# A decoder layer on one core: half of the last pair's value projection moved between that pair's scores, with w_out's loads spread behind its parts

## Chip, cores and metric

One core of one Trainium2 chip. The metric is the device time of one execution in microseconds; three runs of the kernel before gave a median of 2648.34 us (2646.84 to 2651.65).

## What is computed

Per batch of four (1024 tokens, 1024 channels): a layer norm, causal self-attention with 16 heads of 64, a residual; a layer norm and a cross-attention over a context; a residual; a layer norm and a gated low-rank step; a residual. The first part, cut:

```python
qkv = layernorm(x) @ w_qkv                      # 1024 -> 3 x 1024
scores = einsum('bqhd,bkhd->bhqk', q / 8, k)    # causal mask
attn = softmax(scores)
x = x + einsum('bhqk,bkhd->bqhd', attn, v) @ w_out
x = x + cross_attention(layernorm(x), ctx, Wq, bq, Wk, bk)
x = x + gated_low_rank(layernorm(x), ...)
```

## The kernel before, in words

**Work and names.** Heads are taken two at a time: eight pairs p = 0 to 7 per batch, n = 8b + p over all. Each number is split into two fp16 halves, so a product is three matmuls (`three`, lines 559 to 566). Each engine walks a list of steps written out by hand: `PE_BODY` and its like for pairs 0 to 6, `PE_TAIL` and its like for pair 7 and all that follows it in the batch (lines 41 to 93). A `+` behind a step means that it belongs to the next pair (or batch), a `-` to the one before. `walk` (lines 306 to 326) goes through them; `ONCE` adds single steps, among them `JI0 JI1 KI` behind T6 of pair 6 of each batch (line 139).

**The steps spoken of.** `P t h part` is a quarter of a projection (t: 0 query, 1 key, 2 value; h: the half of the tokens; six 512-column matmuls, lines 570 to 592) that reads the turned input `xt` in array `r1`. `CH`/`CL` take the finished bank out of PSUM on ACT (line 776) and DVE (line 914). `V` (lines 455 to 460, SP) is the DMA transpose of the value half-pair rows into `vn`. `S q` are the scores of query block q (PE, lines 608 to 630), `X q` their maximum (DVE, 915 to 928), `E q j` the exponentials of head j (ACT, 792 to 803), `R q` one over their sum (DVE, 929 to 936), `H q j`/`L q j` the two fp16 halves of the probabilities (POOL 1196 to 1204, DVE 937 to 942), `T q` the DMA transpose of block q's probabilities, 4(q+1) blocks of 128x128 (SP, 445 to 454). `M0`/`M1` multiply the turned probabilities with the values, for query blocks 0 to 3 and 4 to 7 (PE, 631 to 653); `OH`/`OL` take the result out. `OI i` loads a quarter (1 MB) of w_out into `wo`, which is the same memory as `xt` (SP, 506 to 513). `KI` loads the cross-attention's weights (512 KB) into memory that is also the projection weights' (SP, 514 to 516); `KH`, `KL` split them (828 to 830, 1100 to 1103). `JI` loads a quarter of the context (512 KB, 517 to 524), `JH`/`JL` split it, `G` projects it (683 to 692), `QH`/`QL` take that out. `B` is the output projection (703 to 720).

**Order around the change.** All DMAs of these steps are issued by SP, one after another, on one queue. In pair 6's body PE ends with `P200+ P201+ P202+ P203+ P210+ P211+ P212+ S0+ S1+ P213+`; SP ends with T6, JI0, JI1, KI, T7, V+. KI waits until all 48 banks of the batch are projected (line 515). In the tail PE goes `S2 S3 M1- S4 G0 S5 G1 M0 S6 G2 B00 S7 ...`, and SP `OI0 OI1 T0 T1 OI2 T2 OI3 JI2 T3 T4 JI3 ...`. The waits that set the order:

```python
sp.wait_ge(part_ok, 6 * PAIRS * (b + 1))      # 507, OI: all banks projected
sp.wait_ge(l_ok, 2 * (TB * n + q) + 2)        # 447, T: both low halves of q
if q >= PARTS + 2: sp.wait_ge(m_ok, 2 * n + 1)
elif q < PARTS and n > 0: sp.wait_ge(m_ok, 2 * n)   # 450-451: M1 of the pair before
pe.wait_ge(t_in[s], 16 * (4 * n + 2 * g + 2)) # 634, M0: T0 to T3; M1: T0 to T7
pe.wait_ge(v_in, 16 * (n + 1))                # 635, M0: this pair's V
```

Of the kernel before, what the change touches and what calls it, by code (L numbers as in the profile page):

```python
# [14 lines left out]
P = 128  # L15
# [13 lines left out]
PARTS = 4  # L29
# [28 lines left out]
"""  # L58

PE_TAIL = """  # L60
    S2 S3 M1- S4 G0 S5 G1 M0 S6 G2 B00 S7 G3 B01 B10 B11 M1 B20 N0 B21 N1 B30 N2 B31 N3 B40 N4 B41 N5 B50 N6 B51 N7
    B60 B61 B70 B71 Z00 Z01 Z10 Z11 Z20 Z21 F0 Z30 Z31 F1 D0 Z40 Z41 F2 D1 U0 Z50 Z51 F3 D2 U1 Z60 Z61 F4 D3 U2
    Z70 Z71 F5 D4 U3 P000+ P001+ P002+ P003+ P010+ P011+ P012+ P013+ F6 D5 U4 P100+ P101+ P102+ P103+ P110+ P111+
    P112+ P113+ F7 D6 U5 P200+ P201+ P202+ P203+ P210+ P211+ P212+ P213+ D7 U6 S0+ S1+ U7
"""
DVE_TAIL = """
    X0 L70- L71- CL21 R0 X1 L00 L01 X2 R1 L10 L11 R2 X3 KL JL0 R3 OL1- X4 L20 L21 QL0 JL1 R4 L30 L31 X5 L40
    L41 QL1 JL2 R5 OL0 X6 L50 L51 R6 QL2 JL3 X7 L60 L61 R7 QL3 RA0 L70 L71 RA1 LB0 OL1 CX0 LL0 LB1 CR0 RA2 CX1 CLO0
    LB2 CR1 CX2 LL1 CLO1 CR2 RA3 CX3 CLO2 LB3 CR3 CX4 CLO3 CR4 RA4 CX5 CLO4 LB4 CR5 CX6 CLO5 CR6 RA5 CX7 CLO6 LB5
    CR7 CLO7 RA6 LB6 AB0+ AB1+ AL0+ RA7 LB7 AL1+  # L70
# [3 lines left out]
    WLO7 Y6 CL21+ Y7  # L74
"""
ACT_TAIL = """
    E00 E01 CH21 E10 E11 E20 E21 KH JH0 E30 E31 OH1- QH0 JH1 E40 E41 E50 E51 QH1 JH2 OH0 E60 E61 QH2 JH3 E70 E71
    QH3 LX0 OH1 CE0 LX1 CE1 CE2 CE3 LX2 CE4 CE5 CE6 CE7 AX0+ AX1+ AX2+ TX0 LX3 AX3+ TX1
    LX4 AX4+ TX2 GE0 LX5 AX5+ TX3 GE1 WHI0 LX6 AX6+ TX4 GE2 WHI1 LX7 AX7+ TX5 GE3 WHI2 TX6 GE4 WHI3 TX7 GE5 WHI4
    CH00+ CH01+ GE6 WHI5 CH10+ CH11+ GE7 WHI6 CH20+ WHI7 CH21+  # L80
# [5 lines left out]
    AH6+ TS4 AS7+ TH4 LH7 AH7+ TS5 TH5 TS6 TH6 TS7 TH7  # L86
"""
SP_TAIL = """
    OI0 OI1 T0 T1 OI2 T2 OI3 JI2 T3 T4 JI3 T5 RI0 T6 RI1 T7 WD0+ WD1+ WD2+ RI2 RI3 CT0 LT0 CT1 RI4
    LT1 RI5 CT2 CT3 RI6 CT4 CT5 RI7 CT6 CT7 AI0+ AI1+ AI2+ AT0+ AT1+ AI3+ LT2 AT2+  # L90
    TT0 AI4+ LT3 AT3+ TT1 AI5+ LT4 AT4+ AI6+ TT2 LT5 AT5+ AI7+ TT3 LT6 YO0 AT6+ TT4 LT7 YO1 AT7+ TT5
    YO2 TT6 YO3 TT7 YO4 WD0++ YO5 WD1++ YO6 V+ YO7
# [58 lines left out]
def decoder_layer(nc, x, w_qkv, w_out, ctx_t, w_ctx, b_ctx, w_ffn, v_ffn, w_up, center, slope, out):  # L151
    es = ExitStack()
    with es:
# [88 lines left out]
        with ExitStack() as s4:  # L242
# [30 lines left out]
        w_ld = [sem(f"w_ld{t}") for t in range(3)]  # L273
        wo_st = [sem(f"wo_st{s}") for s in range(2)]
        part_ok, ch_ok, c_ok, v_in = sems("part_ok ch_ok c_ok v_in")
        s_ok, peak_ok, low_ok, e_ok, den_ok, r_ok, h_ok, l_ok = sems(
            "s_ok peak_ok low_ok e_ok den_ok r_ok h_ok l_ok")
        t_in = [sem(f"t_in{s}") for s in range(2)]
# [26 lines left out]

        def walk(engine, attend, rest):

            for kind, args, off in starts[engine]:
                if kind in OF_PAIR:
                    attend(kind, args, off - 1)  # L310
                else:
                    rest(kind, args, 0)
            for n in range(BATCH * PAIRS):
                b, p = divmod(n, PAIRS)
                for kind, args, off in (tails if p == PAIRS - 1 else bodies)[engine]:
                    if kind in OF_PAIR:
                        m = n + off
                        if p == 0 and off == 0 and kind in ("CH", "CL"):
                            continue
                        if m // PAIRS == b or p == PAIRS - 1 and 0 <= m < BATCH * PAIRS:  # L320
                            attend(kind, args, m)
                    elif b + off < BATCH:
                        rest(kind, args, b + off)
                    if off == 0:
                        for once, which, _ in steps(ONCE.get((engine, n, kind + "".join(map(str, args))), "")):
                            rest(once, which, n // PAIRS)
# [90 lines left out]
        with nc.Block() as block:  # L417

            @block.sync
            def _(sp):  # L420
# [49 lines left out]
                def rest(kind, a, b):  # L470
# [12 lines left out]
                    if kind == "AI":  # L483
                        if b > 0:
                            if i < 2:
                                sp.wait_ge(n_lo, TB * b)
                            else:
                                sp.wait_ge(a_lo, T - 1)
                        sp.dma_start(x_in(T), x[b, i]).then_inc(a_in[T % 2] if b > 0 else a_first[i], 16)
                    elif kind == "AT":  # L490
                        sp.wait_ge(a_lo, T + 1)
                        if b > 0:
                            sp.wait_ge(out_mm, TB * b)
                        sp.dma_start_transpose(xt[:, :, :, :].rearrange("p s k q -> p (s k) q")[:, :, block_of(i)],
                                               xh1[:, T % 2, :, :].rearrange("p s d -> p (s d)")
                                               ).then_inc(xt_in[T % 2], 16)
                    elif kind == "VI":
                        if i == 0:
                            sp.wait_ge(scan_ok, 12)
                        else:  # L500
                            sp.wait_ge(wo_ok, i)
                        sp.dma_start(wo_raw, w_out[i]).then_inc(wo_in, 16)
                    elif kind == "VS":
                        sp.wait_ge(wo_ok, i + 1)
                        sp.dma_start(wo_pairs[:, :, i, :], wo16[:, i % 2, :, :]).then_inc(wo_st[i % 2], 16)
                    elif kind == "OI":
                        sp.wait_ge(part_ok, 6 * PAIRS * (b + 1))
                        if b == 0:
                            for s in range(2):
                                sp.wait_ge(wo_st[s], 64)  # L510
                        sp.dma_start(wo[:, :, 2 * i:2 * i + 2, :].rearrange("p s k d -> p s (k d)"),
                                     wo_pairs[:, :, 2 * i:2 * i + 2, :].rearrange("p s k d -> p s (k d)")
                                     ).then_inc(wo_ld, 16)
                    elif kind == "KI":
                        sp.wait_ge(part_ok, 6 * PAIRS * (b + 1))
                        sp.dma_start(wc_raw[:, :, :, :], w_ctx).then_inc(k_in, 16)
                    elif kind == "JI":
                        if i >= 2:
                            sp.wait_ge(j_ok, 4 * b + i - 1)
                        elif b == 0:  # L520
                            sp.wait_ge(w_ok, 3 * PAIRS)
                        else:
                            sp.wait_ge(y_ok, TB * b)
                        sp.dma_start(ctx_raw[:, i % 2, :, :], ctx_t[b, :, :, i * CQ:(i + 1) * CQ]).then_inc(j_in[i % 2], 16)
                    elif kind == "RI":
                        if i >= 2:
                            sp.wait_ge(x1_ok, T - 1)
                        else:
                            sp.wait_ge(j_ok, 4 * b + 3 + i)
                        sp.dma_start(x_res[:, i % 2, :], x[b, i]).then_inc(xr_in[i % 2], 16)  # L530
                    elif kind == "CT":
                        sp.wait_ge(n_lo, T + 1)
                        sp.wait_ge(m_ok, 2 * PAIRS * (b + 1))
                        sp.dma_start_transpose(at[:, :, :, :].rearrange("p s k q -> p (s k) q")[:, :, block_of(i)],
                                               cn[:, i % 2, :, :].rearrange("p s d -> p (s d)")
                                               ).then_inc(at_in[i % 2], 16)
                    elif kind == "LT":
                        sp.wait_ge(b_lo, T + 1)
                        if i >= 2:
                            sp.wait_ge(xm_ok, T - 1)  # L540
                        sp.dma_start_transpose(t2[:, i % 2, :, :, :].rearrange("p s k t -> p (s k) t"),
                                               xh2.rearrange("p s d -> p (s d)")).then_inc(t2_in, 16)
                    elif kind == "TT":
                        sp.wait_ge(d_lo, T + 1)
                        if i >= 2:
                            sp.wait_ge(f_mm, T - 1)
                        sp.dma_start_transpose(t3[:, i % 2, :, :, :].rearrange("p s k t -> p (s k) t"),
                                               xh3.rearrange("p s d -> p (s d)")).then_inc(t3_in, 16)
                    elif kind == "YO":
                        sp.wait_ge(y_ok, T + 1)  # L550
                        sp.dma_start(out[b, i], x1[:, i, :]).then_inc(y_out, 16)
# [6 lines left out]
            def _(pe):  # L558
# [9 lines left out]
                def attend(kind, a, n):  # L568
                    b, p = divmod(n, PAIRS)
                    if kind == "P":  # L570
# [19 lines left out]
                                   [2 * part, 2 * part + 1], part == 0, part == PARTS - 1)  # L590
                        if part == PARTS - 1:
                            mm.then_inc(part_ok, 1)
                    elif kind == "WC":
                        if n >= PAIRS:
                            return
# [164 lines left out]
            def _(act):  # L760
# [52 lines left out]
                def rest(kind, a, b):  # L813
# [13 lines left out]
                                       scale=rs1[:, i:i + 1]).then_inc(a_xn, 1)  # L827
                    elif kind == "KH":
                        act.wait_ge(k_in, 16 * (b + 1))
                        act.activation(wc_hi[:, :, :, :], wc_raw[:, :, :, :], ACT.Copy).then_inc(kh_ok, 1)  # L830
                    elif kind == "JH":
                        act.wait_ge(j_in[i % 2], 16 * (2 * b + i // 2 + 1))
# [49 lines left out]
            def _(dve):  # L882
# [186 lines left out]
                def rest(kind, a, b):  # L1069
# [29 lines left out]
                        pair_rest(wo16[:, i % 2, 1, :], wo_raw, up_o[:, i:i + 1], wo16[:, i % 2, 0, :], wo_ok)  # L1099
                    elif kind == "KL":  # L1100
                        dve.wait_ge(kh_ok, b + 1)
                        dve.tensor_tensor(wc_lo[:, :, :, :], wc_raw[:, :, :, :], wc_hi[:, :, :, :].bitcast(F32),
                                          ALU.subtract).then_inc(kl_ok, 1)
                    elif kind == "JL":
# [201 lines left out]
```

## Time and profile before

| | |
|---|---|
| median of 3 runs | 2648.34 us |
| the profiled execution's own time | 2649.84 us |
| its span, first to last instruction | 2647.9 us |
| mean granted TensorE clock | 0.965 |
| busy: PE, DVE, ACT, POOL | 2396.1, 1848.5, 816.2, 711.5 us |
| DMA, mean of 16 engines | 66.3% on SP's and ACT's queues' main ring (q1) |

The profile gives busy time by engine and by group of instructions, what ended an engine's idle time, the chain of work that ended last, and the DMA issues. A matmul's row lasts longer than the distance to the next (they are pipelined), so rows of PE are read by their starts. For DMAs the timeline gives the issue on SP (SPq); the time to landing is in the answers on one line of the kernel. Batches are counted 1 to 4 below.

### The profile page before, as it was taken

The numbers are of one execution on the slowest core, as the hardware profiler recorded it, in microseconds if no ns is written. First come the engines' busy times: TensorE is split into PE (matmuls) and PEld (weight loads), VectorE is DVE, ScalarE is ACT, GpSimd is POOL, SyncE is SP. The second block draws the span as 40 slices with busy tenths as digits, with TensorE's granted clock in tenths as the row PEclk, the third lists the DMA queues.
The fourth block names the chain that finished last, engine by engine and source line by source line (L and its number), as shares of the span: only waits on it lengthen the run. The fifth ranks groups of instructions, "written<-read, shape, count | busy, mean of one in ns | idle before, by whom it ended". The sixth has DMA issues, their size and how long they took to land.

```text
span 2647.9 us, 38004 instructions
## 1 busy us (share of the span) xinstructions
PE 2396.1 (90%) x14411; PEld 1175.2 (44%) x14411; DVE 1848.5 (70%) x3423; ACT 816.2 (31%) x1629; POOL 711.5 (27%) x981
## 2 busy tenths in 40 slices
PE   4888888799989999899898999979988999988996
PEld 2334343454444444454453444444444444435444
DVE  5677887657957776756876767775695777765576
ACT  2454333322123333321213333331221333342110
POOL 3332443124212222213411222222430222221220
PEclk9999999899999999899998999989998999999997
DMA  7687778856547777866745777686663677776543
GB/s 213 162 213 172 174 183 181 206 142 145 126 101 146 144 143 145 187 150 147 151 104 118 142 149 144 131 205 156 147 131 94 136 146 145 143 162 171 112 80 96
DMA packets 983130, 393.49 MB, mean 149 GB/s; under 512 B 936796, under 2 KB 946012, under 8 KB 982948
## 3 DMA queue, kind: packets, MB, share of 16 engines
q1 hardware_dynamic: 980356, 381.63, 66.3%
q10 hardware_dynamic: 2592, 9.44, 1.1%
q8 instruction: 114, 1.87, 0.3%
q14 instruction: 68, 0.56, 0.1%
HBM read 122.56 MB, written 33.55 MB: 59 GB/s over the span
## 4 chain that ended last, share of the span: by engine, by line
PE 59%; DVE 20%; DMA 8%; issue 7%; ACT 3%; POOL 3%; SPq 1%; ACTq 0%; POOLq 0%; DVEq 0%
PE ps_p L563 8%; PE ps_p L565 8%; PE ps_p L564 8%; DMA r<-pn 7%; PE ps_s L563 7%; PE ps_s L565 7%; PE ps_s L564 7%; PE ps_s L623 6%; PE ps_o L650 5%; DVE pn L884 5%; DVE peak L924 2%; ACT probs L802 2%; DVE bn L889 2%; PE ps_s L628 1%; POOL pn L1174 1%
## 5 line engine op out<-in xcount | busy, mean ns | idle before, releaser
L1174 POOL TENSOR_SCALAR pn<-probs,rden 128x640 f16<-128x640 f32 (+7 forms) x512 | 396.4, 787 | 1260.0 <-DVE rden L936 763.0
L802 ACT ACTIVATE probs<-ps_s,low,sizes 128x640 f32<-128x640 f32 (+7 forms) x512 | 421.2, 826 | 865.0 <-DVE low L927 752.9
L884 DVE SCALAR_TENSOR_TENSOR pn<-probs,rden,pn 128x640 f16<-128x640 f32 (+7 forms) x512 | 461.3, 937 | 153.4 <-POOL pn L1174 151.9
L563 PE MATMUL ps_p<-r,w 128*128 128x512 f16 x1344 | 516.4, 384 | 3.5 <-DVE qk L884 3.5
L564 PE MATMUL ps_p<-r,w 128*128 128x512 f16 x1344 | 515.5, 384 | 0.0
L565 PE MATMUL ps_p<-r,w 128*128 128x512 f16 x1344 | 515.0, 383 | 0.0
L623 PE MATMUL ps_s<-qk 64*128 64x512 f16 (+3 forms) x2304 | 245.7, 340 | 122.9 <-ACT probs L802 112.3
L924 DVE TENSOR_REDUCE peak<-ps_s 128x2 f32<-128x1280 f32 (+3 forms) x128 | 241.6, 1887 | 93.6 <-PE ps_s L628 91.0
L650 PE MATMUL ps_o<-r,vn 128*64 128x512 f16 (+3 forms) x2304 | 210.4, 339 | 31.4 <-issue 31.1
L623 PEld LDWEIGHTS ps_s<-qk 64*128 64x128 f16 x2304 | 92.0, 97 | 272.0 <-ACT probs L802 147.2
L565 PEld LDWEIGHTS ps_p<-r,w 128*128 128x128 f16 x1344 | 132.9, 99 | 162.9 <-issue 7.8
L563 PEld LDWEIGHTS ps_p<-r,w 128*128 128x128 f16 x1344 | 133.0, 99 | 143.5 <-issue 5.5
L563 PE MATMUL ps_s<-r,pn 128*128 128x512 f16 x512 | 194.7, 380 | 0.0
L564 PE MATMUL ps_s<-r,pn 128*128 128x512 f16 x512 | 194.4, 380 | 0.0
L565 PE MATMUL ps_s<-r,pn 128*128 128x512 f16 x512 | 194.3, 379 | 0.0
L564 PEld LDWEIGHTS ps_p<-r,w 128*128 128x128 f16 x1344 | 133.0, 99 | 137.9 <-issue 5.1
L650 PEld LDWEIGHTS ps_o<-r,vn 128*64 128x64 f16 x2304 | 132.4, 113 | 125.0 <-issue 65.1
L563 PE MATMUL ps_s<-r 128*128 128x512 f16 x384 | 145.9, 380 | 0.0
L564 PE MATMUL ps_s<-r 128*128 128x512 f16 x384 | 145.5, 379 | 0.0
L565 PE MATMUL ps_s<-r 128*128 128x512 f16 x384 | 145.5, 379 | 0.0
L1178 POOL TENSOR_SCALAR ve<-mv 128x1 f32<-128x1 f32 x96 | 28.5, 297 | 400.1 <-DVE mv L892 398.7
L933 DVE TENSOR_SCALAR den_s<-den 128x2 f32<-128x2 f32 x256 | 42.5, 166 | 114.3 <-ACT probs L802 114.1
(189 smaller groups left out, 3546.2 us busy)
## 6 DMA issues: line engine op xcount, KB each, us to landing
w<-w_pairs SPq DMA_DIRECT2D x72, 512.0 KB, 4.0
r<-wo_pairs SPq DMA_DIRECT2D x16, 1024.0 KB, 6.6
w_raw<-in_x SPq DMA_DIRECT2D x32, 512.0 KB, 4.2
out<-r SPq DMA_DIRECT2D x32, 512.0 KB, 2.9
w_pairs<-w SPq DMA_DIRECT2D x24, 512.0 KB, 7.1
qk<-in_x SPq DMA_DIRECT2D x24, 512.0 KB, 4.5
w_raw<-in_ctx_t SPq DMA_DIRECT2D x16, 512.0 KB, 5.0
w_raw<-in_w_qkv ACTq DMA_DIRECT2D x12, 512.0 KB, 6.3
```

The lines of the kernel that those rows point to most:

```text
L563: pe.matmul(ps, lh, rh, start=start and k == ks[0], stop=False)
L564: pe.matmul(ps, lh, rl, start=False, stop=False)
L565: mm = pe.matmul(ps, ll, rh, start=False, stop=stop and k == ks[-1])
L623: pe.matmul(ps_s[:, j, to.start + c:to.start + d], qk_part(n, 0, qs, block_of(q))[rows(j), :], qk_part(n, 1, ks, slice(c, d))[rows(j), :], ...
L650: mm = pe.matmul(ps_o[rows(j), g, c:HALF], vn[:, n % 2, vs, kb, rows(j)], keys_of(g, j, s, kb), start=kb == 0 and vs == 0 and s == 0, stop ...
L802: act.activation(probs_part(q, j, w), ps_s[:, j, scores(q)], ACT.Exp, bias=low[:, n % 2, i:i + 1], scale=sc(n), accum_out=den[:, n % 2, i: ...
L884: dve.scalar_tensor_tensor(out=to, in0=bank, scalar=scale, in1=rounded, op0=ALU.mult, op1=ALU.subtract).then_inc(ok, 1)
L889: ins = dve.bn_stats(bn[:, T % 2, h, :], src[:, half(h)])
L924: dve.tensor_reduce(peak[:, n % 2, r], ps_s[:, :, scores(q)], AX_X, ALU.max).then_inc(peak_ok, 1)
L933: dve.tensor_scalar(den_s[:, n % 2, r], den[:, n % 2, r], 1.0 / UP_A, None, ALU.mult).then_inc(den_ok, 1)
L1174: pool.tensor_scalar(to, src, scale, 1.0, ALU.mult, ALU.mult).then_inc(ok, 1)
L1178: pool.tensor_scalar(ve, mv[:, 1:2], EPS, UP_X ** -2, ALU.add, ALU.mult).then_inc(ok_ve, 1)
```

## The change

The four parts P210 to P213 of pair 7 leave pair 6's body: the walk skips them there, and the tail has them around S2 and S3. V of pair 7 leaves the end of pair 6's list on SP and stands behind OI3 in the tail. T0 stands ahead of OI0, T1 between OI0 and OI1. Each of OI0 to OI2 waits for the part of P21 that has read its memory last (a new semaphore), OI3 for all banks. CH21 and CL21 move back, KI waits for the query banks only, and KH and KL take over the rest of its wait.

```diff
 PE_TAIL = """
-    S2 S3 M1- S4 G0 S5 G1 M0 S6 G2 B00 S7 ...
+    P210 S2 P211 P212 S3 P213 M1- S4 G0 S5 G1 M0 S6 G2 B00 S7 ...
 DVE_TAIL = """
-    X0 L70- L71- CL21 R0 X1 L00 L01 X2 R1 L10 L11 R2 X3 KL JL0 R3 OL1- X4 ...
+    X0 L70- L71- R0 X1 L00 L01 X2 R1 L10 L11 R2 X3 CL21 KL JL0 R3 OL1- X4 ...
 ACT_TAIL = """
-    E00 E01 CH21 E10 E11 E20 E21 KH JH0 E30 E31 OH1- ...
+    E00 E01 E10 E11 E20 E21 KH JH0 CH21 E30 E31 OH1- ...
 SP_TAIL = """
-    OI0 OI1 T0 T1 OI2 T2 OI3 JI2 T3 T4 JI3 T5 ...
+    T0 OI0 T1 OI1 OI2 T2 OI3 V JI2 T3 T4 JI3 T5 ...
...
+        xt_free = sem("xt_free")
...
                 for kind, args, off in (tails if p == PAIRS - 1 else bodies)[engine]:
+                    if p == PAIRS - 2 and off == 1 and (kind == "V" or kind == "P" and args[:2] == (2, 1)):
+                        continue
...
                     elif kind == "OI":
-                        sp.wait_ge(part_ok, 6 * PAIRS * (b + 1))
+                        if i < PARTS - 1:
+                            sp.wait_ge(xt_free, 3 * b + i + 1)
+                        else:
+                            sp.wait_ge(part_ok, 6 * PAIRS * (b + 1))
...
                     elif kind == "KI":
-                        sp.wait_ge(part_ok, 6 * PAIRS * (b + 1))
+                        sp.wait_ge(part_ok, 6 * PAIRS * (b + 1) - 4)
...
                         if part == PARTS - 1:
                             mm.then_inc(part_ok, 1)
+                        elif p == PAIRS - 1 and (t, h) == (2, 1):
+                            mm.then_inc(xt_free, 1)
...
                     elif kind == "KH":
                         act.wait_ge(k_in, 16 * (b + 1))
+                        act.wait_ge(part_ok, 6 * PAIRS * (b + 1) - 2)
...
                     elif kind == "KL":
                         dve.wait_ge(kh_ok, b + 1)
+                        dve.wait_ge(part_ok, 6 * PAIRS * (b + 1))
```

## Rows read from the trace of the kernel before

**Rows 1.** The page's costliest groups: the scores on PE.

```profile
L623 PE MATMUL ps_s<-qk 64*128 64x512 f16 (+3 forms) x2304 | 245.7, 340 | 122.9 <-ACT probs L802 112.3
```

**Rows 2.** Busy time by stretch: S0 to M0 of pair 7, in the four batches.

```profile
core 0: us, PE busy (x) PEld busy (x) DVE busy (x) ACT busy (x) POOL busy (x), PEclk, DMA share, GB/s
457.90:496.60 38.70, 21.64 (x163) 13.57 (x162) 27.46 (x51) 15.88 (x35) 9.45 (x12) 0.78 1.03 263
1095.70:1131.40 35.70, 22.14 (x163) 13.52 (x162) 25.16 (x49) 15.67 (x34) 7.76 (x12) 0.81 1.02 260
1731.20:1766.20 35.00, 21.55 (x163) 13.17 (x163) 25.14 (x49) 15.56 (x34) 8.25 (x12) 0.80 1.04 267
2366.90:2401.80 34.90, 21.79 (x163) 14.25 (x162) 24.60 (x49) 15.67 (x34) 7.83 (x12) 0.80 1.03 265
```

**Rows 3.** The same view for the 64 us from M0 on, batch 2.

```profile
1131.40:1195.00 63.60, 62.16 (x357) 33.33 (x358) 32.98 (x49) 14.33 (x23) 12.89 (x17) 0.97 0.57 134
```

**Rows 4.** Timeline of PE: pair 6's M1 and pair 7's M0, four batches; last, a later M1.

```profile
470.45 5.95 PE L650 MATMUL ps_o<-r,vn 128*64 128x512 f16 x48 [1.99 <-issue]
1107.02 6.81 PE L650 MATMUL ps_o<-r,vn 128*64 128x512 f16 x48 [2.52 <-issue]
1742.82 6.35 PE L650 MATMUL ps_o<-r,vn 128*64 128x512 f16 x48 [2.78 <-issue]
2378.40 6.00 PE L650 MATMUL ps_o<-r,vn 128*64 128x512 f16 x48 [3.43 <-issue]
...
496.65 2.62 PE L650 MATMUL ps_o<-r,vn 128*64 128x512 f16 x24 [4.08 <-issue]
1131.46 2.55 PE L650 MATMUL ps_o<-r,vn 128*64 128x512 f16 x24 [3.57 <-issue]
1766.21 2.43 PE L650 MATMUL ps_o<-r,vn 128*64 128x512 f16 x24 [3.15 <-issue]
2401.87 3.18 PE L650 MATMUL ps_o<-r,vn 128*64 128x512 f16 x24 [2.22 <-issue]
...
1166.07 4.41 PE L650 MATMUL ps_o<-r,vn 128*64 128x512 f16 x48
```

**Rows 5.** Timeline of SP's queue, batch 2 (L459 is V, L511 are the OIs).

```profile
1098.30 0.35 SPq L516 DMA_DIRECT2D wc_raw<-in_w_ctx  x1
1099.65 5.43 SPq L454 DMA_TRANSPOSE r<-pn  x1
1105.18 2.07 SPq L459 DMA_TRANSPOSE vn<-vt  x1
1107.30 1.53 SPq L511 DMA_DIRECT2D r<-wo_pairs  x2
1113.90 2.56 SPq L454 DMA_TRANSPOSE r<-pn  x2
```

**Rows 6.** Busy time by stretch, batch 2: first only a transpose moves, then only w_out.

```profile
1101.70:1104.70 3.00, 1.79 (x8) 0.41 (x8) 1.63 (x6) 2.49 (x9) 0.00 (x0) 0.50 1.25 208
1110.00:1114.00 4.00, 4.00 (x40) 2.41 (x38) 2.88 (x6) 1.77 (x5) 0.00 (x0) 0.76 1.00 392
```

**Rows 7.** The view by line, L511 (16 OIs, all batches): issue to landing.

```profile
DMA to landing us min/median/max: 5.3/6.6/8.3
```

**Rows 8.** The same view, L454 at 1699.6 us: a T0 with nothing queued ahead.

```profile
DMA to landing us min/median/max: 2.4/2.4/2.4
```

**Rows 9.** Timeline of PE and DVE before S0, batch 2, and ACT's E71.

```profile
1095.76 0.34 PE L623 MATMUL ps_s<-qk 64*128 64x128 f16 x6
...
1094.33 0.20 ACT L802 ACTIVATION_READ_ACCUMULATOR probs<-ps_s,low,sizes 128x1 f32 x1
...
1095.04 0.69 DVE L884 SCALAR_TENSOR_TENSOR vt<-ps_p,vt 128x512 f16<-128x512 f32 x1
1096.36 0.29 DVE L920 TENSOR_REDUCE peak<-ps_s 128x1 f32<-128x128 f32 x1 [0.63 <-PE ps_s L628]
```

**Rows 10.** Timeline of POOL, batch 1: H20 waits for T0's landing.

```profile
482.69 2.11 POOL L1174 TENSOR_SCALAR pn<-probs,rden 128x384 f16<-128x384 f32 x3 [11.25 <-DMA r<-pn]
```

More of the change, by code:

```diff
@@ L60 @@
 PE_TAIL = """
-    S2 S3 M1- S4 G0 S5 G1 M0 S6 G2 B00 S7 G3 B01 B10 B11 M1 B20 N0 B21 N1 B30 N2 B31 N3 B40 N4 B41 N5 B50 N6 B51 N7
+    P210 S2 P211 P212 S3 P213 M1- S4 G0 S5 G1 M0 S6 G2 B00 S7 G3 B01 B10 B11 M1 B20 N0 B21 N1 B30 N2 B31 N3 B40 N4 B41 N5 B50 N6 B51 N7
     B60 B61 B70 B71 Z00 Z01 Z10 Z11 Z20 Z21 F0 Z30 Z31 F1 D0 Z40 Z41 F2 D1 U0 Z50 Z51 F3 D2 U1 Z60 Z61 F4 D3 U2
@@ L66 @@
 DVE_TAIL = """
-    X0 L70- L71- CL21 R0 X1 L00 L01 X2 R1 L10 L11 R2 X3 KL JL0 R3 OL1- X4 L20 L21 QL0 JL1 R4 L30 L31 X5 L40
+    X0 L70- L71- R0 X1 L00 L01 X2 R1 L10 L11 R2 X3 CL21 KL JL0 R3 OL1- X4 L20 L21 QL0 JL1 R4 L30 L31 X5 L40
     L41 QL1 JL2 R5 OL0 X6 L50 L51 R6 QL2 JL3 X7 L60 L61 R7 QL3 RA0 L70 L71 RA1 LB0 OL1 CX0 LL0 LB1 CR0 RA2 CX1 CLO0
@@ L76 @@
 ACT_TAIL = """
-    E00 E01 CH21 E10 E11 E20 E21 KH JH0 E30 E31 OH1- QH0 JH1 E40 E41 E50 E51 QH1 JH2 OH0 E60 E61 QH2 JH3 E70 E71
+    E00 E01 E10 E11 E20 E21 KH JH0 CH21 E30 E31 OH1- QH0 JH1 E40 E41 E50 E51 QH1 JH2 OH0 E60 E61 QH2 JH3 E70 E71
     QH3 LX0 OH1 CE0 LX1 CE1 CE2 CE3 LX2 CE4 CE5 CE6 CE7 AX0+ AX1+ AX2+ TX0 LX3 AX3+ TX1
@@ L88 @@
 SP_TAIL = """
-    OI0 OI1 T0 T1 OI2 T2 OI3 JI2 T3 T4 JI3 T5 RI0 T6 RI1 T7 WD0+ WD1+ WD2+ RI2 RI3 CT0 LT0 CT1 RI4
+    T0 OI0 T1 OI1 OI2 T2 OI3 V JI2 T3 T4 JI3 T5 RI0 T6 RI1 T7 WD0+ WD1+ WD2+ RI2 RI3 CT0 LT0 CT1 RI4
     LT1 RI5 CT2 CT3 RI6 CT4 CT5 RI7 CT6 CT7 AI0+ AI1+ AI2+ AT0+ AT1+ AI3+ LT2 AT2+
```

## The prediction, made before the changed kernel was run

> **What bounds the kernel now.** I read the page first, then the busy time by stretch, the timelines of PE and SP, and the DMA landings. The page lets one expect a gain: PE is the busiest engine, and its costliest idle time is the scores' wait for exponentials [rows 1]. So filling that wait with projection matmuls looks free. The stretches say where such waits lie. From S0 to M0 of the last pair PE is busy 21.6 of 38.7 us in batch 1 and about 22 of 35 in the others, at a granted clock near 0.8. DMA, however, is full all the way (share 1.02 to 1.04) [rows 2]. After M0 it turns round: PE is busy 62.16 of 63.60 us and DMA 0.57 [rows 3]. So what ends the first stretch is what M0 waits for, and every microsecond by which M0 starts later is a microsecond of the kernel, because PE has no slack behind it.
>
> M0 waits for T0 to T3 and V. Its own idle time before is 2.2 to 4.1 us with "issue" as releaser [rows 4], which is here a transfer. M1 of pair 6, the other large wait, needs T7 and starts after 2.0 to 3.4 us of idleness; T0 of pair 7 may only be issued when M1 has ended: in batch 2 M1 ends at 1107.02 + 6.81 = 1113.83 and T0 is issued at 1113.90 [rows 4, 5]. While M1 runs, SP's queue isn't empty before: V was issued at 1105.18 and OI0, OI1 from 1107.30 [rows 5], so the DMA engines carry them under M1's wait.
>
> **Rates of the queue.** A stretch with only transposes moves 208 GB/s, one with only w_out 392 GB/s [rows 6]. A transpose T q is 4(q+1) blocks of 32 KB: 0.6, 1.3, 1.9 and 2.5 us for T0 to T3; V has 16 blocks, 2.5 us; a quarter of w_out (1 MB) is 2.7 us, JI2 (512 KB) 1.3 us. Together what lies between T7 and M0 is 0.6 + 1.3 + 1.9 + 2.5 + 2.5 + 4 x 2.7 + 1.3 = 20.9 us of a queue served in order. Batch 2 spends 1131.46 - 1107.02 = 24.4 us on it, so it is nearly packed.
>
> **The change, part by part.** The lag from M1's end to M0's start is before 20.25, 17.63, 17.04 and 17.47 us (starts and lengths in [rows 4]).
>
> (1) PE ahead of S0. P210 to P212, 18 matmuls 0.216 us apart (18 x 0.216 = 3.9 us), leave. In batch 2 S0 starts at 1095.76 though the last exponential it waits for ended at 1094.53 [rows 9]. It can start 1.2 us sooner; but its maximum on DVE stands behind CL20, which ends at 1095.73, against 1096.36 now. The gain passed on is 0.63 us, up to L70, L71 and T7's issue. The same holds in batches 3 and 4; in batch 1 DVE, busy with a step of w_out's split, gives nothing. Bounds 0 and 1.2 us; I take 0.63 in three batches.
>
> (2) PE in the tail. 24 matmuls, 5.2 us, now lie before S2 (1.3), before S3 (2.6) and before M1 (1.3). They are covered by the waits for exponentials and for T7's landing: PE is idle some 13 us per batch of this stretch [rows 2]. Without that cover they'd cost 5.2 us a batch. Cost 0.
>
> (3) M1's speed. M1 takes 5.95, 6.81, 6.35 and 6.00 us here and 4.41 us at 1166.07, where nothing idles before it [rows 4]. With P211 to P213 around S3 PE idles for little more than 1 to 2 us before M1, so I take 4.41: gains of 1.54, 2.40, 1.94 and 1.59 us, 7.5 in sum. The other bound is no gain, as a gap still stands before it. The Trainium skill, "TensorE: Matmul & The Clock Gate", Part 1, says that the throttled clock is the default and that activity releases it; by it M1, still behind a gap, might stay slow, and the sum would be 7.5 us higher. No row shows M1 with this filling ahead.
>
> (4) SP's order. SP now reaches T0 right after T7 and stands there until M1 ends; OI0 to OI3 and V are behind it on the engine. The new semaphore of OI0 to OI2 is thus satisfied long before it is looked at, and V, whose data is ready before, comes after OI3. So V and OI0, OI1 (2.5 + 5.4 us), carried under M1 before, are now paid for after it. The new lag: T0's issue 1.3 us with the step to the next, OI0's landing at least 5.3 us from its own issue [rows 7], then OI1 to OI3 8.0, T1 1.3, T2 1.9, V 2.5, JI2 1.3, T3 2.5, wait 0.1: 24.2 us. The other end: T0 lands 2.4 us after its issue [rows 8], and the other 20.3 us follow without a gap: 22.7. Between them I take 23.5, near the middle, since batch 2's 24.4 us for the same work still hold gaps. T3's own condition (L31) isn't late: E40 stands behind G0's chain at about M1's end plus 6 us, L31 at some 12, T3's turn at 21.
>
> (5) T0 lands alone, in 2.4 us in place of up to 6: in batch 1 H20 waited until 482.69, 6.3 us behind M1's end [rows 4, 10]. E40, S5, G1 come earlier by that, and then stand before M0. Gain at M0: 0.
>
> (6) CL21 (0.69 us, [rows 9] for its like) leaves the place before X1 and lands before KL, where DVE waits for OH1; CH21 falls into ACT's wait for X3. KI may go 3 us sooner, in front of T7 in the queue as before, 1.3 us of transfer: between 0 and 0.6 us for T7, taken 0. KH's and KL's new waits are satisfied when P213 is done, ahead of M1. Together 0; if CL21 held OL1 up it would cost 0.7 us to G0, which isn't on M0's path.
>
> **Sum.** M1 now ends at 470.45 + 4.41 = 474.86; 1107.02 - 0.63 + 4.41 = 1110.80; 1746.60; 2382.18. Plus 23.5, M0 starts at 498.36, 1134.30, 1770.10 and 2405.68: later by 1.7, 2.8, 3.9 and 3.8, in sum 12.2 us. The profiled execution's 2649.84 becomes 2662.0; the median shown is 1.5 us below it, so the forecast for the median is 2648.34 + 12.2 = 2660.5. Lags of 22.7 and 24.2 give +9.0 and +15.0; M1 not faster adds 7.5; M0 and its 10.8 us (four times, [rows 4]) all at half clock, 4 x 3.64, would add 3.8.
>
> **Rivals.**
> (A) M1 stays slow, since PE still idles before it: all of (4) without (3), +19.7, 2668. For it: each M1 and M0 behind a gap was slow. Against: the gap shrinks.
> (B) The queue packs better, and the lag is 20.25 us in each batch, batch 1's of before, which also had T0 late: -1.5, -0.4, +0.6, +0.5, sum -0.8: 2647.5, no change. Against: 20.25 is under the queue's 20.9 us of work; it needs faster transposes than those rows.
> (C) Faster. The queue is no bound; M0 follows M1 by the same lag as before, since other steps (E40, S5, L31) set it and these come earlier with T0. Then (1) and (3) are kept: -(7.5 + 1.9) = -9.4, 2639. Its place is the wait before M0; it decides if T3 lands within 17 to 20 us of M1's end, and from a lag under 21 the sum turns negative. For it: DMA share is measured over packets that overlap (it reads above 1), so it could overstate the load. Against: the GB/s agree with it.
> (D) Hidden: the extra wait is made up behind M0. Against: PE 62.16 of 63.60 [rows 3]. I count it with B.
>
> **Chances.** Forecast 0.47; A 0.2; B with D 0.19; C 0.14. A measurement of this kernel tells about 0.2%, 5.3 us, from no change. A and the forecast lie above it: slower 0.67, same 0.19, faster 0.14. The range reaches from B's case with 1.5 us to spare, 2646, to A with the upper lag, 2672; C and the half-clock M0 stay out. The likely case's own range is 2657 to 2664.
>
> **What would show it.** Right: M1 of pair 6 at 4.4 us; T0 as the first issue after T7, at M1's end; V issued behind OI3; M0 22.7 to 24.2 us behind M1's end with a longer idle time; DMA share well below 1 under M1. Wrong: a lag below 21, or M0 released by something other than V and T3; PE gaps behind M0 that shrink by what M0 lost; P211 to P213 pushing S3 back.

## Result, and the profile after

The changed kernel takes 2672.94 us (median of 5 runs, 2670.35 to 2676.31) beside 2649.65 us for the kernel before in the same five rounds (2646.84 to 2656.59). The ratio is 1.007, with an interval of 1.0056 to 1.0085: slower by 0.7%, some 18 us by the interval's middle and 23 us by the medians. The forecast was 2660.5 us, slower, in a range of 2646 to 2672. The sign was forecast, and the size was between half and two thirds of the measured one: 12.2 us beside 23 or 18. The median lies 0.9 us above the range's upper end as given; by the ratio, 1.007 on the 2648.34 us that the forecast started from, it is 2667 us. Either figure is above the likely case's own range, 2657 to 2664, and closer to rival A's 2668 than to the forecast.

The first view is the busy time by stretch of the kernel after: S0 to M0 of the last pair in the four batches, then M1's run alone and M1's end to M0's start in batch 2, and last the 64 us from M0 on.

```profile
core 0: us, PE busy (x) PEld busy (x) DVE busy (x) ACT busy (x) POOL busy (x), PEclk, DMA share, GB/s
458.20:500.10 41.90, 26.41 (x182) 15.81 (x184) 28.06 (x52) 15.91 (x35) 8.89 (x12) 0.76 0.89 242
1102.70:1143.80 41.10, 24.39 (x182) 14.98 (x183) 27.66 (x51) 15.90 (x35) 7.95 (x12) 0.86 0.81 229
1740.60:1782.10 41.50, 24.51 (x180) 15.12 (x181) 27.57 (x51) 15.89 (x35) 7.93 (x12) 0.86 0.82 228
2382.60:2423.80 41.20, 24.40 (x182) 14.97 (x183) 27.75 (x51) 15.99 (x35) 7.93 (x12) 0.86 0.82 229
...
1114.50:1120.60 6.10, 6.10 (x50) 3.92 (x52) 5.49 (x10) 1.63 (x5) 0.93 (x2) 0.72 0.02 5
1120.60:1143.80 23.20, 9.94 (x78) 7.65 (x76) 14.36 (x22) 7.95 (x15) 4.09 (x6) 0.82 0.97 289
...
1143.80:1207.40 63.60, 62.22 (x353) 33.17 (x354) 32.31 (x48) 14.32 (x23) 12.19 (x16) 0.96 0.56 135
```

Compare [rows 2]: the stretches have grown from 35 us to 41 and more in batches 2 to 4 (in batch 2 1.1 us of it because S0 starts sooner after pair 6's M0), and the DMA share has fallen from between 1.02 and 1.04 to 0.81 or 0.82 there, and to 0.89 in batch 1. The two rows of batch 2 show where it fell. While M1 runs the queue moves 5 GB/s at a share of 0.02; from M1's end to M0 it is at 0.97. PE does more in the stretch (24.39 us in place of 22.14), as was wanted, and the stretch is longer all the same. After M0 nothing gives way: 62.22 of 63.60 us, [rows 3] again.

The timeline of SP's queue in batch 2 (L460 transposes probabilities, L520 loads w_out, L465 is V, L533 the context):

```profile
1107.68 14.15 SPq L460 DMA_TRANSPOSE r<-pn  x2
1121.89 0.59 SPq L520 DMA_DIRECT2D r<-wo_pairs  x1
1122.57 1.27 SPq L460 DMA_TRANSPOSE r<-pn  x1
1123.90 1.32 SPq L520 DMA_DIRECT2D r<-wo_pairs  x2
1125.32 5.44 SPq L460 DMA_TRANSPOSE r<-pn  x1
1130.81 0.59 SPq L520 DMA_DIRECT2D r<-wo_pairs  x1
1131.50 5.98 SPq L465 DMA_TRANSPOSE vn<-vt  x1
1137.53 0.59 SPq L533 DMA_DIRECT2D w_raw<-in_ctx_t  x1
1138.21 6.75 SPq L460 DMA_TRANSPOSE r<-pn  x2
```

The first row merges T7 and T0: between them SP waits for M1, with nothing issued, where [rows 5] have V and two quarters of w_out. V is now issued at 1131.50 and its issue holds SP for 5.98 us, where the same issue took 2.07 us before the change [rows 5]; T3 follows at 1138.21. I read the longer issue as SP held up by what is queued ahead of V; no run isolates it. And PE's M1 of pair 6 and M0 of the last pair, in its timeline:

```profile
470.92 4.41 PE L661 MATMUL ps_o<-r,vn 128*64 128x512 f16 x48 [0.69 <-issue]
1114.46 6.10 PE L661 MATMUL ps_o<-r,vn 128*64 128x512 f16 x48 [1.99 <-issue]
1752.43 6.10 PE L661 MATMUL ps_o<-r,vn 128*64 128x512 f16 x48 [2.06 <-issue]
2394.44 6.10 PE L661 MATMUL ps_o<-r,vn 128*64 128x512 f16 x48 [1.98 <-issue]
...
500.07 3.42 PE L661 MATMUL ps_o<-r,vn 128*64 128x512 f16 x24 [8.48 <-DMA r<-pn]
1143.79 3.41 PE L661 MATMUL ps_o<-r,vn 128*64 128x512 f16 x24 [9.29 <-DMA r<-pn]
1782.10 3.41 PE L661 MATMUL ps_o<-r,vn 128*64 128x512 f16 x24 [9.50 <-DMA r<-pn]
2423.79 3.41 PE L661 MATMUL ps_o<-r,vn 128*64 128x512 f16 x24 [9.30 <-DMA r<-pn]
```

M0 now waits 8.5 to 9.5 us with a transpose as named releaser; before it was 2.2 to 4.1 [rows 4]. The lag from M1's end to M0's start is 24.74, 23.23, 23.57 and 23.25 us.

### The profile page after: what moved, and what is told of

Read it like the earlier page. It is cut to its first block, busy times and chain, and to the rows that moved or that the text cites. A ratio compares the mean times of both kernels' runs of the same rounds, so it can differ in the third digit from the quotient of the medians.

```text
span 2670.8 us, 38012 instructions
## 1 busy us (share of the span) xinstructions
PE 2402.3 (90%) x14411; PEld 1177.9 (44%) x14411; DVE 1850.2 (69%) x3423; ACT 816.0 (31%) x1629; POOL 710.3 (27%) x981
## 4 chain that ended last, share of the span: by engine, by line
PE 56%; DVE 20%; DMA 11%; issue 6%; POOL 3%; ACT 3%; SPq 1%; ACTq 0%; POOLq 0%; DVEq 0%
DMA r<-pn 10%; PE ps_p L572 8%; PE ps_p L573 8%; PE ps_p L574 8%; PE ps_s L572 7%; PE ps_s L573 7%; PE ps_s L574 7%; DVE pn L896 5%; PE ps_s L634 5%; PE ps_o L661 4%; DVE peak L936 3%; ACT probs L813 2%; DVE bn L901 2%; POOL pn L1187 1%; PE ps_s L639 1%
## 5 line engine op out<-in xcount | busy, mean ns | idle before, releaser
L634 PE MATMUL ps_s<-qk 64*128 64x512 f16 (+3 forms) x2304 | 245.8, 340 | 119.5 <-ACT probs L813 109.3
```

What stands on the lines that cost most here:

```text
L634: pe.matmul(ps_s[:, j, to.start + c:to.start + d], qk_part(n, 0, qs, block_of(q))[rows(j), :], qk_part(n, 1, ks, slice(c, d))[rows(j), :], ...
```

## Experiments

Seven kernels, each timed in five rounds beside the kernel before, whose median was 2654.01 us in the rounds of 1 to 4 and 2652.15 us in those of 5 to 7. That is 4.4 and 2.5 us above its 2649.65 us of the result, so the times in us are read through the ratios. The theory, called queue: the 20.9 us of transfers between T7 and M0 bound the stretch, so that whatever isn't sent while M1 runs is paid for ahead of M0. The rival, called PE: the moved matmuls, with the idle time and the clock that they leave behind, cost it.

**1. T0 behind the transfers again.** On the changed kernel, OI0, OI1 and V ahead of T0. (Before the change V stood ahead of OI0, at the end of pair 6's list.)

```diff
-    T0 OI0 T1 OI1 OI2 T2 OI3 V JI2 T3
+    OI0 OI1 V T0 T1 OI2 T2 OI3 JI2 T3
```

> The changed kernel with only SP's order in the tail put back: OI0 OI1 V T0 T1 OI2 T2 OI3 JI2. The moved value projection, CH21, CL21 and KI stay as changed. Theory queue (what costs is that SP's queue stands empty while pair 6's M1 runs): the two quarters of w_out and V go out under M1 again, the lag from M1's end to M0's start returns from 23.2 to 24.7 us to about 17 to 18.5 (batch 1 up to 20), and the time comes back to 2645 to 2652 us. Rival PE (the moved matmuls, the idle time before S0 and the clock cost it): the lag stays and so does the time, 2668 to 2675 us.

Measured: 2658.22 us beside 2654.01, ratio 1.0016 (1.0004 to 1.0029). Most of the loss is gone with not one matmul moved back; the rival's 2668 us is out. But the queue theory's figures were missed too. The time is above 2652 us, and the lag from M1's end to M0's start is 22.82, 20.37, 18.77 and 19.89 us, where 17 to 18.5 and up to 20 in batch 1 were expected. The timeline of batch 2 (SP, then POOL and DVE, then PE) has the rest:

```profile
1113.65 1.24 SPq L520 DMA_DIRECT2D r<-wo_pairs  x2
1119.55 3.67 SPq L465 DMA_TRANSPOSE vn<-vt  x1
1123.31 2.57 SPq L460 DMA_TRANSPOSE r<-pn  x2
...
1115.60 0.93 POOL L1187 TENSOR_SCALAR pn<-probs,rden 128x256 f16<-128x256 f32 x2 [6.29 <-DMA r<-pn]
1116.11 1.09 DVE L896 SCALAR_TENSOR_TENSOR pn<-probs,rden,pn 128x256 f16<-128x256 f32 x2 [4.72 <-POOL pn L1187]
1118.84 0.68 DVE L896 SCALAR_TENSOR_TENSOR vt<-ps_p,vt 128x512 f16<-128x512 f32 x1
...
1115.54 4.41 PE L661 MATMUL ps_o<-r,vn 128*64 128x512 f16 x48 [2.47 <-issue]
```

V's data are ready only with CL21 at 1118.84 + 0.68. CL21 stands behind L10, L11, R2 and X3 on DVE. L10 waits for H10 on POOL (1115.60), and H10 for a transpose's landing, which is T7's: it was issued at 1108.25 and landed 7.2 us later. SP issues V at 1119.55 and is held until 1123.2, though M1 ended at 1119.95: T0 is 3.4 us late. So the move of P213 has a price of its own, and it too is paid in the queue.

**2. The opposite: the kernel before with T0 first.**

```diff
-    OI0 OI1 T0 T1 OI2 T2 OI3 JI2 T3
+    T0 OI0 T1 OI1 OI2 T2 OI3 JI2 T3
```

> The kernel before with only SP's tail reordered: T0 OI0 T1 OI1 OI2 T2 OI3; V stays at the end of pair 6's list, and all projections stay where they were. Theory queue: V still goes out under M1, the 5.3 us of OI0 and OI1 come after it: the lag grows by 3.5 to 5 us a batch, the time to 2663 to 2669 us. Rival PE: no change from the kernel before, 2647 to 2653 us.

Measured: 2667.43 us, ratio 1.0046 (1.0026 to 1.0065). No projection is moved here, and a large part of the loss is there. The rival expected no change. The lag grew by 1.0, 3.5, 3.5 and 2.9 us, less than the 3.5 to 5 expected of the queue; the time fell into its range, 2663 to 2669, but in rounds in which the kernel before was 4.4 us slower (by the ratio it is some 2662 us).

**3. V ahead of T0**, w_out's quarters behind, on the changed kernel:

```diff
-    T0 OI0 T1 OI1 OI2 T2 OI3 V JI2 T3
+    V T0 OI0 T1 OI1 OI2 T2 OI3 JI2 T3
```

> The changed kernel with V ahead of T0 (V T0 OI0 T1 OI1 OI2 T2 OI3): V's 2.5 us of transfer lie under M1, the quarters of w_out behind it as changed. Theory queue: a lag about 2.5 us shorter than the changed kernel's, about 21 us in batches 2 to 4, and 10 us off the time: 2660 to 2666 us. Rival PE: 2668 to 2675 us.

Measured: 2664.86 us, ratio 1.0041 (1.0028 to 1.0054). The lag is 23.59, 20.84, 23.21 and 22.31 us; the 21 us expected came in batch 2 alone. V isn't ready when SP reaches it: in batch 2 it is issued at 1111.75, 4 us into M1.

**4. OI0 and OI1 ahead of T0**, V behind OI3:

```diff
-    T0 OI0 T1 OI1 OI2 T2 OI3 V JI2 T3
+    OI0 OI1 T0 T1 OI2 T2 OI3 V JI2 T3
```

> The changed kernel with OI0 and OI1 ahead of T0 as before the change, V still behind OI3. Theory queue: 5.3 us of w_out lie under M1, V's 2.5 us stay after it: lag about 19 to 20.5 us in batches 2 to 4, the time 2653 to 2660 us. Rival PE: 2668 to 2675 us.

Measured: 2660.96 us, ratio 1.0022 (1.0008 to 1.0037). Of the two transfers that the change took from under M1, putting back the longer one (5.3 us) gives back more than putting back V (2.5 us, and late, see 1), as the theory has it: M1 to M0 takes 104.8 us in sum here and 109.3 in 3. The intervals of the two ratios overlap, so the order of 3 and 4 is clear in the profiles and not in the times.

**5. V ready early.** The move kept, but P213 ahead of S3 and CL21 ahead of L10, and SP's order as before the change:

```diff
-    P210 S2 P211 P212 S3 P213 M1-
+    P210 S2 P211 P212 P213 S3 M1-
-    R1 L10 L11 R2 X3 CL21 KL
+    R1 CL21 L10 L11 R2 X3 KL
-    E20 E21 KH JH0 CH21 E30
+    E20 E21 CH21 KH JH0 E30
-    T0 OI0 T1 OI1 OI2 T2 OI3 V JI2 T3
+    V OI0 OI1 T0 T1 OI2 T2 OI3 JI2 T3
```

> The changed kernel with P213 ahead of S3, CL21 ahead of L10, CH21 behind E21, and SP's tail as V OI0 OI1 T0 T1 OI2 T2 OI3 JI2: the value half still lies between the last pair's scores, but V is ready before T7 lands and goes out under M1. Theory queue (what the first series left of the loss was V, not ready until CL21 and then in T0's way): from M1's start to M0's start 23.5 to 24.5 us as before the change, M1's start 0.6 us earlier in three batches, and the time is that of the kernel before or up to 3 us less, a ratio of 0.998 to 1.001. Rival PE (the moved matmuls cost something by themselves, as idle time before S0 or as a later S3): as the first series' best order, 1.001 to 1.003.

Measured: 2653.41 us beside 2652.15, ratio 1.0002 (0.9992 to 1.0012). No loss is left that these runs can tell, with the value half still between the scores. In batch 2 V goes out under M1 again (SP's queue, then PE):

```profile
1105.02 1.99 SPq L465 DMA_TRANSPOSE vn<-vt  x1
1107.06 1.62 SPq L520 DMA_DIRECT2D r<-wo_pairs  x2
1110.72 2.79 SPq L460 DMA_TRANSPOSE r<-pn  x2
...
1106.24 4.41 PE L661 MATMUL ps_o<-r,vn 128*64 128x512 f16 x48 [2.00 <-issue]
1130.95 3.41 PE L661 MATMUL ps_o<-r,vn 128*64 128x512 f16 x24 [3.63 <-issue]
```

M1 is 2.4 us shorter than before the change (4.41 for 6.81), and yet M0 starts 24.71 us behind M1's start, against 24.44 then [rows 4]. The queue has been full meanwhile, at a share of 1.07 from 1107 to 1120; for 1 us then, at 1120, just as T2 is issued, it falls to 0.23. With the queue as bound a faster M1 buys nothing; I take this as the reason why the move, cleared of its costs, gains nothing either. Of M1 to M0, 23.5 to 24.5 us were expected and 26.30, 24.71, 25.76 and 23.97 came: the ratio was as forecast, the stretch in three batches longer.

**6. Less ahead of T3.** If the queue bounds the stretch of the kernel before, taking 4 us of transfers that M0 doesn't need from ahead of T3 must make it faster:

```diff
-    OI0 OI1 T0 T1 OI2 T2 OI3 JI2 T3 T4 JI3
+    OI0 OI1 T0 T1 OI2 T2 T3 JI2 OI3 T4 JI3
```

> The kernel before with only JI2 and OI3 moved behind T3 on SP (T2 T3 JI2 OI3 T4): less work lies ahead of T3 in the queue, all else as before. Theory queue: T3 is issued at its own condition (L31, some 10 us behind M1's end) and lands about 5 us later, M0 starts 1 to 2.5 us sooner in each batch, the ratio is 0.996 to 0.999. Rival: JI2, then late, holds JH2 and with it X6, or OI3 holds B00, and the ratio is 0.999 to 1.002.

Measured: 2641.48 us beside 2652.15, ratio 0.9956 (0.9938 to 0.9973), faster than both kernels. M0 in batch 2:

```profile
1133.59 1.82 PE L650 MATMUL ps_o<-r,vn 128*64 128x512 f16 x24 [0.27 <-issue]
```

Its wait has shrunk from 3.57 to 0.27 us and, PE no longer idle, it runs in 1.82 us. Over the four batches M0 starts 2.2 to 3.1 us sooner after M1's start, where 1 to 2.5 were expected.

**7. 5 and 6 together.**

```diff
-    T0 OI0 T1 OI1 OI2 T2 OI3 V JI2 T3 T4 JI3
+    V OI0 OI1 T0 T1 OI2 T2 T3 JI2 OI3 T4 JI3
```

with the other three lists as in 5.

> Both together: the value half between the scores with V ready early, and JI2 and OI3 behind T3. Theory queue: with 4 us of transfer taken from ahead of T3, M0 follows the softmax of blocks 2 and 3 and no longer the queue, so that an earlier and faster M1 counts as well: 1 to 3 us sooner in each batch, a ratio of 0.995 to 0.998. Rival: as for the one before, 0.999 to 1.002.

Measured: 2642.42 us, ratio 0.9961 (0.9946 to 0.9976), no better than 6. PE's timeline in batch 2 shows no idle time before M0; the wait that is left is that of the scores of S5, ahead of M0 in PE's list, for an exponential:

```profile
1125.37 2.10 PE L634 MATMUL ps_s<-qk 64*128 64x512 f16 x12 [3.83 <-ACT probs L813]
...
1132.19 1.82 PE L661 MATMUL ps_o<-r,vn 128*64 128x512 f16 x24
```

The queue isn't M0's last wait there any more, yet the moved value half still brings nothing that these runs can tell. The expectation that an earlier and faster M1 would now count isn't borne out.

All of it in one table. The second column is the time from M1's start to M0's start, summed over the four batches of one profile (in the kernel before 26.20 + 24.44 + 23.39 + 23.47); the third is its excess over the kernel before as a share of 2650 us, the last what the rounds gave.

| kernel | M1 to M0, us | share | ratio, interval |
|---|---|---|---|
| before | 97.5 | | |
| changed | 117.5 | +0.75% | 1.007 (1.0056 to 1.0085) |
| 3, V first | 109.3 | +0.45% | 1.0041 (1.0028 to 1.0054) |
| 2, before, T0 first | 108.3 | +0.41% | 1.0046 (1.0026 to 1.0065) |
| 4, OIs first | 104.8 | +0.28% | 1.0022 (1.0008 to 1.0037) |
| 1, T0 behind again | 101.2 | +0.14% | 1.0016 (1.0004 to 1.0029) |
| 5, V ready early | 100.7 | +0.12% | 1.0002 (0.9992 to 1.0012) |
| 7 | 87.3 | -0.39% | 0.9961 (0.9946 to 0.9976) |
| 6, T3 early | 86.5 | -0.42% | 0.9956 (0.9938 to 0.9973) |

The stretch ahead of M0 alone orders the kernels almost without fault (2 and 3 change places), and its share lies within each interval or at its edge. Two things limit this. Kernels 1 and 5 differ by 0.5 us here and by more in their ratios. And each profile is one execution, whose span also has the spread of the rest: that of 6 is its slowest run, 2650.11 us, and its span of 2648.3 us is no shorter than the 2647.9 of the kernel before. The gain of 6 rests on the ratio of its runs.

## Why the prediction was right, and where its size was off

Take the stretch from M0 of pair 6 to M1 of the last pair in both profiles; over four batches it grew from 357.5 to 378.2 us, by 20.7. The remaining 2.2 us of the two spans' 22.9 lie elsewhere, in pieces of both signs, and I leave them open: from M1 of the last pair of batch 1 to M0 of pair 6 in batch 2 it is 4.4 us more, in the same stretch between batches 2 and 3 2.8 us less. Experiment 6, which doesn't touch those stretches either, has 5.0 us more in the first. The 20.7 us split by the steps of the prediction:

- **(1) PE ahead of S0**: M1 starts 0.04, 0.60, 0.78 and 0.76 us sooner after M0 of pair 6, together 2.2; forecast 1.9. Right in size, batch 1 included, where nothing was expected.
- **(2) PE in the tail** at cost 0: right. P211 to P213 push nothing that ends the stretch; experiment 5 with all of them ahead of S3 shows it best.
- **(4) SP's order**: the lag grew by 4.5, 5.6, 6.5 and 5.8 us, together 22.4; the forecast, 23.5 us in each batch, made that 21.6. This was the step that decided, and it held: SP stood at T0, the queue was empty under M1, V and two quarters were paid for afterwards. The bounds, 22.7 and 24.2, hold for three batches; batch 1 is at 24.7.
- **(3) M1's speed** is the term that was mis-sized. I took 4.41 us in all batches, 7.5 us of gain; it was 4.41 in batch 1 and 6.10 in the others, 2.4 us of gain. That is rival A in three batches out of four, and A's +19.7 us, to which I gave 0.2, is nearer to the measured 20.7 than my 12.2. Adding up doesn't show that a faster M1 would have saved the 5.1 us: in batch 1, where M1 did take 4.41 us, M1's start to M0's start is 29.15 us, beside 29.33 to 29.67 in the others. The sentence of the Trainium skill put beside this step, "TensorE: Matmul & The Clock Gate", Part 1 (the throttled clock is the default, activity releases it), pointed the right way here: with 2 us of idle time ahead M1 ran at a granted clock of 0.72. It doesn't settle the matter, as M1 with the same idle time ahead took 4.41 us in other runs (last section).
- **M0's speed**, taken at no cost and priced at up to 3.8 us: M0 is 3.41 or 3.42 us four times, and M0 to M1 grew by 0.21, 0.87, 0.88 and 0.87 us, 2.8 in sum. This isn't M0 alone: M0 grew by 0.80 us in batch 1 and by 0.23 in batch 4, and the scores behind it share the slow clock. The granted clock from M0 to M1 is 0.95 in all batches before and 0.93 in batches 2 to 4 after. I kept this beside the sum. The forecast lag of 23.5 us meant a wait of some 9 us ahead of M0 in batch 2 (23.5 - 17.63 + 3.57), so it should have been in the sum.

So 12.2 us were forecast; the two clock terms add 5.1 and 2.8, the lag 0.8, and (1) takes 0.3: 20.6, and 20.7 before rounding. Rivals B and D fell with the lag and with PE's 62.22 of 63.60 us behind M0. Rival C fell with the lag too, and with experiment 2 above all: T0 did land in its 2.4 us, and in the changed kernel's batch 1 H20 came 2.65 us behind M1's end in place of 6.3, and it was worth nothing while V and T3 were late.

**(5)**, that T0 alone gains nothing at M0, and **(6)**, CL21's move at no cost, are different. (5) held. (6) held only because V was made late by its place on SP anyway: once SP's order is put back, CL21's place behind X3 costs V its slot and T0 3.4 us in the batch shown (experiment 1), and moving it ahead of L10 clears that (experiment 5). I had costed CL21 by G0 and not by V, which waits for it.

## To carry over

Where a DMA queue served in order is full, count what it carries while the engines wait for something else: an issue put first that itself has to wait (here T0, for M1) empties the queue for as long, and much of that comes back at the next wait that needs the queue's last transfer. In the changed kernel the queue was idle for 21.7 us of the four M1s (by their DMA shares of 0.19, 0.02, 0.00 and 0.01) and the lag grew by 22.4; in experiment 2 it was 14.4 us (0.67, 0.32, 0.34 and 0.41), and the lag grew by 10.9. Filling an engine's idle time gains nothing where that engine isn't what ends the stretch; taking transfers that the wait doesn't need from ahead of it (here JI2 and OI3, 4 us) gained 0.4%. A step that is moved also moves those that only its result releases, and they may sit on another engine's queue.

## What the runs showed beyond that

M1 of pair 6 comes in two speeds once matmuls stand right ahead of it. In the three kernels without matmuls right ahead of it (before, 2, 6) it took 5.74 to 7.25 us in all 12 cases. In the six with P211 to P213 around or ahead of S3 it took 4.41 us in 13 of 24 cases and 6.09 or 6.10 in the other 11, 5, 4, 2 and 2 of the six in batches 1 to 4. The granted clock goes with it; the changed kernel's four M1s:

```profile
470.92:475.33 4.41, 4.41 (x48) 3.06 (x48) 3.76 (x9) 0.98 (x3) 0.93 (x2) 1.00 0.19 71
1114.46:1120.56 6.10, 6.10 (x50) 3.92 (x52) 5.45 (x10) 1.63 (x4) 0.93 (x2) 0.72 0.02 5
1752.43:1758.53 6.10, 6.10 (x50) 3.89 (x52) 5.46 (x10) 1.63 (x4) 0.93 (x2) 0.72 0.00 0
2394.44:2400.54 6.10, 6.10 (x50) 3.86 (x52) 5.45 (x10) 1.63 (x4) 0.93 (x2) 0.72 0.01 3
```

Here the fast one has 0.69 us of idle time ahead and the slow ones 2. But the idle time alone doesn't decide it: in experiment 3 M1 took 6.10 us after 2.12 us of it and 4.41 after 2.03, 1.94 and 1.90. What does, no run here shows.
